# Who copies the gather indices in a graph network's edge loops: GpSimd between its gathers, or VectorE once per step

## What is computed

```python
def _gcn_conv(x, row, col, edge_w, W, b, num_nodes):
    ...
    msg = xw[r] * norm[:, None]
    out = jax.ops.segment_sum(msg, c, num_segments=num_nodes)
...
e = _ln(_mlp(edge_feat, edge_enc_w0, ...), edge_enc_g, edge_enc_beta)
for s in range(S):                      # S = 2
    ce = jnp.concatenate([e, n[senders], n[receivers]], axis=-1)
    e = e + _ln(_mlp(ce, edge_blk_w0[s], ...), ...)
    agg = jax.ops.segment_sum(e, receivers, num_segments=num_nodes)
    cn = jnp.concatenate([n, agg], axis=-1)
    n = n + _ln(_mlp(cn, node_blk_w0[s], ...), ...)
```

## Time and profile before

| what | value |
|---|---|
| median of 3 runs | 18072.75 us (18071.34 to 18078.55) |
| the profiled execution's own time | 18121.37 us |
| its span in the trace | 18119.2 us |
| GpSimd busy | 14425.3 us, 80% |
| PE busy | 13301.6 us, 73% |
| DVE busy | 9511.5 us, 52% |
| ACT busy | 3049.3 us, 17% |
| gathers in the four edge loops (line 818) | 11,687 |
| index copies on GpSimd (line 821) | 11,687 |

### The profile page before, as it was taken

How to read it: one execution, slowest core, us unless ns; L and a number is a source line. 1 busy time by engine, 2 the same in 40 slices (tenths; PEclk the granted TensorE clock), 3 DMA queues, 4 the chain that set the end, 5 groups by cost and what they waited for, 6 DMA issues and landing times. The chain is left out here.

```text
span 18119.2 us, 353439 instructions
## 1 busy us (share of the span) xinstructions
PE 13301.6 (73%) x95144; PEld 10759.4 (59%) x95144; DVE 9511.5 (52%) x28331; ACT 3049.3 (17%) x5120; POOL 14425.3 (80%) x23987
## 2 busy tenths in 40 slices
PE   3777777777689999976777777767667667667775
PEld 2555555555479999974555555555545555555554
DVE  5444444444378888875445454445554444444444
ACT  1222222222200000001111111111111111111111
POOL 6888888888778888876888888888778888888886
PEclk5555555555589999996777777777776776777776
DMA  3222222222211111113555555555444444444442
GB/s 107 60 61 59 61 60 60 61 59 61 61 37 28 27 27 28 27 24 107 147 148 150 147 149 149 146 148 150 119 117 126 125 124 126 124 125 126 125 125 70
DMA packets 1973701, 1714.60 MB, mean 95 GB/s; under 512 B 1266475, under 2 KB 1436319, under 8 KB 1972431
## 3 DMA queue, kind: packets, MB, share of 16 engines
q10 hardware_dynamic: 939256, 958.97, 16.3%
q0 software_dynamic: 394560, 282.16, 9.7%
q1 hardware_dynamic: 639488, 469.70, 9.2%
HBM read 1096.56 MB, written 615.90 MB: 95 GB/s over the span
## 5 line engine op out<-in xcount | busy, mean ns | idle before, releaser
L818 POOL DMA_INDIRECT s_gt<-ta_d,s_ix x6448 | 6329.1, 982 | 1621.3 <-issue 967.9
L818 POOL DMA_INDIRECT g_gt<-xs_d,g_ix x3224 | 3158.7, 980 | 807.0 <-issue 483.6
L687 DVE TENSOR_TENSOR s_P<-psw,dlT 128x1024 f32<-128x1024 f32 x806 | 987.2, 1225 | 4106.8 <-PE psw L1055 4062.8
L1033 PE MATMUL pair<-ident,s_gt 128*128 128x128 f32 x3224 | 781.5, 389 | 2760.8 <-DMA s_gt<-ta_d,s_ix 2759.7
L1008 PE MATMUL pair<-g_part,g_Oh 128*128 128x224 bf16 x25389 | 2542.2, 261 | 238.9 <-DVE g_sel L851 211.7
L1008 PEld LDWEIGHTS pair<-g_part,g_Oh 128*128 128x128 bf16 x25389 | 2431.8, 99 | 279.4 <-issue 203.8
L1055 PEld LDWEIGHTS psw<-s_R,s_P 128*128 128x128 f32 x12896 | 2118.2, 247 | 734.3 <-issue 734.3
L818 POOL DMA_INDIRECT g_gt<-ys_d,g_ix x2015 | 1990.1, 988 | 583.6 <-POOL g_ix L821 325.6
L1033 PEld LDWEIGHTS pair<-ident,s_gt 128*128 128x128 f32 x3224 | 506.2, 194 | 3016.2 <-issue 1873.4
L1055 PE MATMUL psw<-s_R,s_P 128*128 128x64 f32 x12896 | 1998.8, 323 | 2.2 <-DVE s_R L920 1.4
L1055 PEld LDWEIGHTS psw<-g_R,g_P 128*128 128x128 f32 x6448 | 1405.3, 330 | 612.9 <-issue 612.9
(11 more groups left out here) (333 smaller groups left out, 18150.3 us busy)
## 6 DMA issues: line engine op xcount, KB each, us to landing
s_dl<-dl_d SPq DMA_DIRECT2D x404, 512.0 KB
seg_d<-s_sg ACTq DMA_DIRECT2D x806, 256.0 KB
s_Bw<-tb_d ACTq DMA_DIRECT2D x3224, 48.0 KB
s_Bw<-tb_d SPq DMA_DIRECT2D x3224, 48.0 KB
seg_d<-g_sg ACTq DMA_DIRECT2D x403, 320.0 KB
z_d<-g_rT ACTq DMA_DIRECT2D x403, 256.0 KB
s_z<-z_d ACTq DMA_DIRECT2D x403, 256.0 KB, 2.8
s_gt<-ta_d,s_ix POOLq DMA_INDIRECT x6448
```

Of the source, the lines that this page charges most:

```text
L687: return eng.tensor_tensor(P[:, :, :], bc(columns.rearrange("p (o e) -> p o e", o=1), [128, G, 128]), bc(dlT[:, bass.ds(j * G, G)].rearran ...
L818: eng.indirect_dma_start(out=gt[k][:, s, :], out_offset=None, in_=table[:, :], in_offset=bass.IndirectOffsetOnAxis(ap=ix[k][:, s:s + 1], a ...
L1033: eng.matmul(ps[k][:, 128 * q:128 * q + 128], rows[:, 128 * q:128 * q + 128], ident[:, :], start=q == 0, stop=False, is_transpose=True, sk ...
```

## The change

VectorE copies all 8 columns of an item's indices in one instruction, first thing in its step, three items ahead of the step's number; before it, it waits that the gather that used this buffer last (five items back) has landed. The first three items' indices it copies ahead of the loop. GpSimd copies nothing any more. At the start of its step it waits for VectorE's count `v_ix` and, as before, for `p_pre` or `v_msg`; its wait for its own copy and its wait for an earlier landing are gone. In g2 the copy brings 8 columns although 5 are gathered.

```diff
@@ pool(eng)
                         if stage(j, L_GA):
                             k = (b - L_GA) % 8
-                            if expand:
-                                done(eng, p_pre, j, L_GA + 8)
-                            else:
-                                done(eng, v_msg, j, L_GA + 8)
-                            done(eng, g_ix, j, L_GA)
-                            landed(eng, s_g, GA, i, b, L_GA + 7)
+                            done(eng, v_ix, j, L_GA)
+                            done(eng, p_pre if expand else v_msg, j, L_GA + 8)
                             settle(eng, s_m[1])
                             for s in range(GA):
                                 eng.indirect_dma_start(out=gt[k][:, s, :], ...ix[k][:, s:s + 1]...).then_inc(s_g[k].sem, 16)
-                                last = eng.tensor_copy(ix[(k + 1) % 8][:, s:s + 1], srcT[:, bass.ds((j - L_GA + 1) * G + s, 1)])
-                            last.then_inc(g_ix.sem, 1)
-                    eng.tensor_copy(ix[0][:, 0:GA], srcT[:, 0:GA]).then_inc(g_ix.sem, 1)
@@ dve(eng)
                     eng.tensor_copy(columns, iow[:, :])
+                    for k in range(3):
+                        eng.tensor_copy(ix[k][:, :], srcT[:, k * G:k * G + G]).then_inc(v_ix.sem, 1)
...
+                    def indices(j, b):
+
+                        eng.tensor_copy(ix[(b + 3) % 8][:, :], srcT[:, bass.ds((j + 3) * G, G)]).then_inc(v_ix.sem, 1)
+
                     def step(j, i, b):
+                        if stage(j, 0):
+                            landed(eng, s_g, GA, i, b, 5)
+                            indices(j, b)
                         if mlp and summed and stage(j, L_SUM):
```

More of the change, by code:

```diff
@@ L699, in build @@
         s_m = [ctx.enter_context(nc.semaphore(f"e_mark{b}")) for b in range(2)]
-        g_ix, s_blank = mark("e_gix"), mark("e_blank")
+        v_ix, s_blank = mark("e_vix"), mark("e_blank")
         s_g, s_z, s_so, s_ro, s_dl = [[mark(f"e_{n}{b}") for b in range(m)]
@@ L1077, in edge_loop @@
                     m.passed(NIST)
-                g_ix.passed(NIST + 1)
+                v_ix.passed(NIST + 3)
                 for m in (a_h, p_pre, p_x, a_sq, v_ln) if mlp else ():
```

## The result

The median is 16118.3 us (16116.59 to 16121.84, 4 runs) against 18072.04 before: a ratio of 0.8919, 95% interval 0.8903 to 0.8934, so 10.8% faster. The forecast was 16,150 in a range from 15,990 to 16,600. The profiled execution took 16117.8 us with a span of 16116.0; that of the kernel before had taken 18121.37, 49 us above its median, so differences between the two traces are some 49 us larger than those between the medians.

A forecast was written before the change was run, and what follows sets the result against it. GpSimd's gather stream was taken as the bound in g1, s0 and s1. Savings of 564, 588, 592 and 189 (g2), 1933 us, less 4 give 16192 profiled; 48.6 off for the median: 16,150 us, range 15,990 to 16,600.

The forecast's parts named there:

- Part 1: Removing GpSimd's index copies saves 0.083 us a gather, 0.67 us per step of 8, not their full 0.19 us.
- Part 2: At a step's start GpSimd's 0.66 us wait for its own last copy vanishes wholly; bounds 0 to 0.66 kept.
- The once-a-turn 0.85 us: Extra idle time before GpSimd's second gather once in 8 steps, 0.11 us a step, taken to vanish.
- Part 3: GpSimd's new wait for VectorE's index copy costs nothing within steps, some 40 us to spare; 1 us at each loop's start.
- Part 4: VectorE's added index copy costs it 0.1 us a step (bounds 0 to 0.17), off the path in g1, s0, s1.
- The stretches: Small delays to GpSimd's gathers, including any from VectorE's copy, put at 0.06 us a step in g1, s0, s1.
- g2 at 7.00: In g2 the bound passes to VectorE's step; the pace falls from 7.47 to 7.00 us a step, saving 189 us.
- Rivals A: At a step's start the increment itself keeps the 0.66 us: 798 us in 1209 steps, 16,990 us; chance 5%.
- B: Gathers stay near their old pitch, stretched by VectorE's work: 16,800 us, or 16,500 by the skill's rule; chance 9%.
- C: PE becomes the bound in s0 and s1 at its lower clock, 0.34 us a step, 274 us: 16,420; chance 8%.
- E: The gap between gathers grows to 0.35 us and 0.66 us at a step's start remains: no change; chance 2%.
- rival D: Slower: GpSimd and VectorE wait on each other in a ring 8 items long; 18,650 us at 96 us round; 3%.

The follow-up runs named there:

- experiments 1 to 3: Kernel before, GpSimd still copying: eight copies, two items ahead, 16,969 us; one wide copy, one ahead, 17,186 us; one wide copy, two ahead, 16,184 us.
- experiment 1: Kernel before, with GpSimd's eight index copies made two items ahead instead of one: 16,969 us.
- experiment 2: Kernel before, with one wide GpSimd copy of 8 columns in place of eight narrow ones, still one item ahead: 17,186 us.
- Experiment 8: Changed kernel, with VectorE copying the indices of item j-3 in step j and none ahead of the loop: 18,162 us.
- experiment 7: Changed kernel, with VectorE copying the indices of item j in step j and none ahead of the loop: 16,100 us.
- experiments 4 and 6: Changed kernel with one extra unused fp32 VectorE copy per step of g1: 128x2048, 16,374 us; 128x1024, 16,171 us.
- experiment 5: Changed kernel with one extra unused 128x512 fp32 VectorE copy per step of g1: 16,108 us.

## Why the prediction was right, step by step

- **The bound.** GpSimd's stream of gathers set the pace in g1, s0 and s1, and still does: a pace of 10.00 to 10.02 with a pitch of 1.25. Shown by experiments 1 to 3, which change only GpSimd and come within 20 us of the times expected from the sums.
- **Part 1, 0.67 us a step for the copies.** Right, from the earlier trace rows. Between experiment 1 and the changed kernel the eight copies are worth 0.68 us a step of g1; in experiment 2 seven of them are worth 0.62, where 7 x 0.083 is 0.58.
- **Part 2, the self-wait taken at 0, not 0.66.** Right. Experiment 1 isolates it, and its increment 8.0 us ahead of the gathers shows the lead that the prediction had inferred from the end of g1. The Trainium skill has the order of things (Perfetto Trace Analysis, "DMA Instruction — SWDGE (GPSIMD)"): the sequencer fetches on as soon as it has pushed a gather into the wait queue. The trace agrees, with its 7.4 us of lead.
- **The once-a-turn 0.85 us taken at 0.** Right, experiment 1 has none either.
- **Part 3, the new waits.** Right: GpSimd waits 25 us in all on line 867 in s0 and s1. Experiment 8 shows that the ring was described rightly, and experiment 7 that 5 items are enough within the loops. The microsecond put down for each loop's start did not come: the first gathers of g1, g2 and s1 follow what goes before as closely as they did, within 2 us.
- **Part 4, 0.1 us for VectorE's copy.** Measured: 0.16 us long, 0.07 exposed.
- **The stretches, 0.06 us a step.** Too large: 0.00 to 0.02. By the loops' first gathers g1, s0 and s1 gave 57 us more than the sum had. For the 67 ns of line 1162, from which the bound came, no run has a cause.
- **g2 at 7.00.** VectorE's messages come 6.98 us apart, so the pace was right, and g2 gave 201 us where the sum had 189. Part of that is luck: the 7.0 is the mean of two steps, 6.77 and 7.24. The 0.1 us that was to come back from VectorE's other work is about 0.05, from 6.26 us busy a step (839.02 us by 133.9 steps) to 6.21 without the exposed copy; it nearly cancels the 0.07 that the copy costs.
- **The step to the median.** I took off the 48.6 us by which the profiled execution of before stood above its median. The changed kernel's profiled execution is at its median (16117.8 and 16118.3), so this term should have been 0; why the one execution of before was longer is not known. The trace came out 74 us below its forecast of 16,192 (57 from the stretches, 12 from g2, 4 from the loops' starts). That the median is only 32 us off is luck: the 48.6 us ran against these.
- **The weight given to the port.** I let the 3 ns between mean and median speak "at most faintly" for a lock. That was a wrong reading of the mechanism, though not of the sum: a copy from SBUF to SBUF does hold up a gather, until 0.12 us behind the copy's end in experiments 4 and 6. The Trainium skill (SBUF — State Buffer, "SBUF: two separate sides") gives about 115 ns for this. The price of 348 us worked out from it, 0.29 us a step, did not come. The index copy of 0.16 us is shorter than the one of 0.43 us, which cost nothing in experiment 5; there a gather loses time only to a copy that ends later than about 0.82 us behind the gather's start. So the small mean excess in the earlier trace rows need not mean that there is no lock; it fits a kernel in which no long copy of this kind ends late in a gather.
- **Rivals A, B, C, E** are out by the pace of 10.00 to 10.02. C in particular: PE in s0 is busy 73% at a granted clock of 0.82, in s1 74% at 0.74, and still waits for rows in both.
- **A sign that was off.** PE's wait for gathered rows was to fall to some 2 us a step; it is 2.56 (2065.0 over 806 steps). The 2 us go with 8.12 us of work in a step of s0. PE now does it in 0.728 x 10.02 = 7.3, at a granted clock of 0.82 in place of 0.74, so it waits longer; in s1 its busy share of a step fell to 7.4 us too, at about the old clock, and for that no run has a cause.
- **Two sums that don't come out of their terms.** The likeliest case's upper end, with 133, 81 and 73 us on 16,150, is 16,437 and not 16,400; rival D at 12.0 us a step in three loops is 18,495, or 18,684 with g2 as before, and not 18,650. The forecast rests on neither.

## What to carry to other kernels

To price an instruction that is to be taken out of a stream, look for a place in the trace where the same stream runs without it: 11,687 copies of 0.19 us looked like 2.2 ms and were worth 0.85 (16,969 to 16,118 us), and the larger part of the gain, 1.1 ms, was a wait for an engine's own last instruction, which cost the sequencer its lead once a step. Let such a wait be on something two steps old, and it is free whichever engine does the work. A wait handed to another engine makes a ring; count its items and its way round, since the same edit at a distance of 2 items took back the whole gain (18,162 us).

## What the runs showed that I had not expected

- A VectorE copy of fp32 from SBUF to SBUF that begins 0.1 to 0.5 us after a gather's start holds that gather until 0.12 us behind the copy's own end. On average that costs nothing for a copy of 0.43 us, 0.13 us for 0.69 and 0.66 for 1.23. The copy is not held up by the gather that started first: all 403 copies of 2048 columns took 1.226 to 1.229 us. A 1.22 us comparison with an operand in PSUM costs the gathers nothing.
- A gather of 944 ns takes 976 (the median of experiment 1) behind a copy by GpSimd itself, even when that copy is not waited for.
- In g2 the pace differs by 0.15 us a step, 60 us in all, between two kernels with the same instructions in the loop and GpSimd's gathers starting at another point of VectorE's step; VectorE's bf16 one-hots are 315 against 335 ns. That the point of start does this is argued, not isolated.
